# Two attention loops: ScalarE copies every sum, the shift rows lie on 16 partitions, the odd steps' maxima are turned in the 21st unit, and the next step's scores are not held back

## What is computed

```
q = layer_norm(latents) @ Wq
k, v = split(concat([layer_norm(context), layer_norm(latents)], axis=1) @ Wkv)
weight = softmax(q @ k.T * scale)      # the second layer masks some of the 1601 context rows
out = (weight @ v) @ Wout
x = x + out
```

## Time and profile before

| what | value |
|---|---|
| profiled execution, device time | 2073.62 us |
| its span, first to last instruction | 2071.9 us |
| around the span | 1.7 us |
| TensorE busy | 1933.7 us, 93% |
| VectorE busy | 1679.5 us, 81% |
| ScalarE busy | 1238.3 us, 60% |
| GpSimd busy | 858.2 us, 41% |
| granted TensorE clock, mean over the span | 0.972 |

### The profile page before, as it was taken

The page is one execution under the profiler, slowest core; times in us unless marked ns, Lnnn a source line. Parts: engine busy times, 40 slices in busy tenths (PEclk is TensorE's granted clock), DMA queues, the critical chain, the costliest instruction groups (busy, mean ns, idle before and its releaser), DMA issues. The chain is left out here.

```text
span 2071.9 us, 34568 instructions
## 1 busy us (share of the span) xinstructions
PE 1933.7 (93%) x12154; PEld 1052.6 (51%) x12154; DVE 1679.5 (81%) x3987; ACT 1238.3 (60%) x2218; POOL 858.2 (41%) x926
## 2 busy tenths in 40 slices
PE   7899999999999999889898999999999999999886
PEld 6444545444454544533666544454545454544575
DVE  6789898898989897599656888878797979785657
ACT  4366666666657576444224676868777777776212
POOL 4586565666656651088001414343232323231014
PEclk9899999999999999989998999999999999999898
DMA  4322322222222220133105011121121211110100
GB/s 120 108 74 60 92 80 68 67 68 67 67 67 79 51 67 1 32 109 109 40 1 126 14 38 39 42 47 38 38 45 36 55 38 38 38 30 1 29 1 11
DMA packets 148853, 110.51 MB, mean 53 GB/s; under 512 B 120892, under 2 KB 136232, under 8 KB 148680
## 3 DMA queue, kind: packets, MB, share of 16 engines
q1 hardware_dynamic: 148680, 108.31, 19.2%
HBM read 65.15 MB, written 14.29 MB: 38 GB/s over the span
## 5 line engine op out<-in xcount | busy, mean ns | idle before, releaser
L1256 DVE TENSOR_TENSOR x_p_lo<-x_psum,x_p_hi 128x512 f16<-128x512 f32 (+1 forms) x864 | 584.9, 684 | 113.0 <-ACT x_psum L1023 112.1
L1022 ACT ACTIVATE x_p_hi<-x_psum 128x512 f16<-128x512 f32 (+1 forms) x448 | 268.2, 599 | 263.9 <-PE x_psum L857 214.0
L1022 ACT ACTIVATE x_p_hi<-x_psum,x_bcol 128x512 f16<-128x512 f32 (+1 forms) x416 | 290.0, 697 | 152.0 <-PE x_psum L857 150.1
L883 PE MATMUL x_psum<-x_p_hi,x_x_both 128*128 128x512 f16 (+1 forms) x832 | 317.3, 381 | 30.4 <-DVE x_p_lo L1256 29.5
L855 PE MATMUL x_psum<-x_q,x_xT_both 128*128 128x512 f16 x832 | 317.3, 381 | 4.1 <-DMA x_q<-x_shift_rows 4.1
L857 PE MATMUL x_psum<-x_q,x_xT_both 128*128 128x512 f16 x832 | 316.6, 381 | 0.0
L856 PE MATMUL x_psum<-x_q,x_xT_both 128*128 128x512 f16 x832 | 316.6, 380 | 0.0
L884 PE MATMUL x_psum<-x_p_lo,x_x_both 128*128 128x512 f16 (+1 forms) x832 | 315.8, 380 | 0.0
L885 PE MATMUL x_psum<-x_p_hi,x_x_both 128*128 128x512 f16 (+1 forms) x832 | 315.6, 379 | 0.0
L1195 DVE CUSTOM_DVE_ANT_0 x_junk<-x_psum,x_brow 128x512 bf16<-128x512 f32 (+2 forms) x512 | 279.8, 586 | 9.2 <-PE x_psum L941 7.1
L1198 DVE TENSOR_REDUCE x_mx<-x_psum 128x1 f32<-128x512 f32 (+2 forms) x512 | 276.8, 584 | 4.4 <-PE x_psum L941 3.4
(11 more groups left out here) (473 smaller groups left out, 3517.0 us busy)
## 6 DMA issues: line engine op xcount, KB each, us to landing
x_x_both<-context_rows SPq DMA_DIRECT2D x32, 832.0 KB, 5.4
context_rows<-x_x SPq DMA_DIRECT2D x16, 832.0 KB, 3.5
x_raw<-in_ctx SPq DMA_DIRECT2D x16, 768.0 KB
ssm_c_row<-ssm_bc_rows SPq DMA_DIRECT2D x16, 512.0 KB, 4.2
ssm_b_wide<-ssm_bc_rows SPq DMA_DIRECT2D x7, 512.0 KB, 3.5
x_mrow<-in_mask_BxS_bk SPq DMA_DIRECT2D x16, 200.1 KB
x_Wkv<-in_L_xattn_Wkv SPq DMA_DIRECT2D x4, 512.0 KB, 5.1
x_xT_both<-context_rows SPq DMA_TRANSPOSE x96, 4.0
```

Of the source, the lines that this page charges most:

```text
L883: pe.matmul(out, v_hi, p_hi[r][rows, :], start=start, stop=False)
L1022: act.activation(p_hi[r][rows, :], score[r][rows, :], ACT.Exp, scale=SCORE_UNIT, **bias).then_inc(p_hi_ready, 1)
L1256: v.tensor_tensor(p_lo[r][rows, :], score[r][rows, :], p_hi[r][rows, :], ALU.subtract).then_inc(p_lo_ready, 1)
```

## The change

Four things, all inside `attention_loop`.

1. The copies of sums on VectorE (lines 1273 and 1221) go to ScalarE. Both halves of `sum_c` are copied one after the other at the end of a step, behind the products of units 24 and 25, and the latents' sums in two copies of one bank each, behind the exponentials of units 1 and 2.
2. The shift rows lie on 16 partitions of 128 columns, not on 8 of 256. For that `m8` is made twice side by side, and each of the two DMAs per step (constants out, shift rows in) becomes two of half the size.
3. `TURN_BY` is `LAST` - 6 in place of `LAST` - 4. By the rule in `items` an odd step then has two `max` items in units 6 and 7, one in each of units 8 to 19, and `turn` in unit 20. The even step's table is the same as before.
4. The next step's scores 0, 1 and 2 are issued in units 24, 25 and 26, one in each, ahead of the products.

```diff
-    HOLD = 2
-    TURN_BY = LAST - 4
+    TURN_BY = LAST - 6
...
             def rows_in(at):
                 sp.wait_ge(shift_ready, at.n + 1)
-                sp.dma_start(row_of(q_all[at.npar]), shift_rows[:, :, :, :].rearrange("c s h k -> c (s h k)")).then_inc(shift_in, 16)
+                for s in range(2):
+                    sp.dma_start(row_of(q_all[at.npar], s), side(shift_rows, s)).then_inc(shift_in, 16)
...
-                    elif at.has_next and u > LAST - AHEAD + HOLD:
-
-                        k = u + AHEAD - STEPS
-                        for k in range(0 if k == HOLD else k, k + 1):
-                            scores(k, at.npar, at.half + STEPS, at.n, at.ni)
+                    elif at.has_next:
+                        scores(u + AHEAD - STEPS, at.npar, at.half + STEPS, at.n, at.ni)
...
+            def latents_sums(done, par, k):
+                act.wait_ge(pv_done, done)
+                act.activation(sum_l[:, 8 * k:8 * k + 8, par, :], aux[:, k * HALF:(k + 1) * HALF].rearrange("p (h l) -> p h l", l=L),
+                               ACT.Copy).then_inc(aux_free, 1)
...
                     probabilities(u, at)
+                    if at.b and u in (1, 2):
+                        latents_sums(at.half, 1 - at.par, u - 1)
...
-                act.wait_ge(pv_done, at.half + 2 * KT - 1)
-                act.activation(sum_c[:, 0:8, at.par, :], acc[0].rearrange("p (h l) -> p h l", l=L), ACT.Copy).then_inc(sum_out, 1)
+                for k, done in enumerate((sum_out, sum_out1)):
+                    act.wait_ge(pv_done, at.half + 2 * KT - 1 + k)
+                    act.activation(sum_c[:, 8 * k:8 * k + 8, at.par, :], acc[k].rearrange("p (h l) -> p h l", l=L), ACT.Copy).then_inc(done, 1)
...
                         v.wait_ge(aux_free, at.free(item))
-                        v.tensor_reduce(m8[:, :], mx[:, :, :], AX.X, ALU.max).then_inc(m_ready, 1)
+                        for s in range(2):
+                            v.tensor_reduce(m8[:, s, :], mx[:, :, :], AX.X, ALU.max).then_inc(m_ready, 1)
...
-                    if u == 1 and not (at.first and at.par == 0):
-                        latents_sums(at.half, 1 - at.par)
```

More of the change, by code:

```diff
@@ L563, in attention_loop @@
     warm = sb("warm", [P, 1])
-    mx, m8 = sb("mx", [P, NC_, 4]), sb("m8", [P, NC_])
-    const_rows = sb("const_rows", [NC_, 2, 2, P], F16)
-    shift, shift_rows = sb("shift", [NC_, 2, P]), sb("shift_rows", [NC_, 2, 2, P], F16)
+    mx, m8 = sb("mx", [P, NC_, 4]), sb("m8", [P, 2, NC_])
+    const_rows = sb("const_rows", [2 * NC_, 2, P], F16)
+    shift, shift_rows = sb("shift", [2 * NC_, P]), sb("shift_rows", [2 * NC_, 2, P], F16)
     if masked:
@@ L760, in load_mask, with row_of, side @@
                 sp.dma_start(mcol[par][0:TAIL, CT:KT], one[CT * P:S].rearrange("(p o) -> p o", o=1)).then_inc(mask_in[par], 16)
-            def row_of(q):
-                return q[P - 1:P, :, :]
+            def row_of(q, s):
+                return q[P - 1:P, :, 2 * P * s:2 * P * (s + 1)]
+            def side(rows, s):
+                return rows[NC_ * s:NC_ * (s + 1), :, :].rearrange("c h k -> c (h k)")
             def rows_out(at):
@@ L950, in aux_item @@
                         keep_clock(pe, aux[:, 512:1024], ident, 14)
-                    pe.wait_ge(m_ready, at.n + 1)
-                    ins = pe.transpose(aux[0:NC_, 0:P], m8[:, :], ident[:, :])
+                    pe.wait_ge(m_ready, 2 * at.n + 2)
+                    ins = pe.transpose(aux[0:2 * NC_, 0:P], m8[:, :, :].rearrange("p s c -> p (s c)"), ident[:, :])
                 elif kind == "out":
@@ L1036, in body @@
                     wait_alone(act, sum_parted, 2 * (at.b - 1))
-                act.wait_ge(pv_done, at.half + 2 * KT - 1)
-                act.activation(sum_c[:, 0:8, at.par, :], acc[0].rearrange("p (h l) -> p h l", l=L), ACT.Copy).then_inc(sum_out, 1)
+                for k, done in enumerate((sum_out, sum_out1)):
+                    act.wait_ge(pv_done, at.half + 2 * KT - 1 + k)
+                    act.activation(sum_c[:, 8 * k:8 * k + 8, at.par, :], acc[k].rearrange("p (h l) -> p h l", l=L), ACT.Copy).then_inc(done, 1)
             every(act, before, body)
+            for k in range(2):
+                latents_sums(B * STEPS, 1, k)
         @block.gpsimd
@@ L1200, in consume @@
                     if a == (10 if isinstance(at, Pre) else 1 if at.npar else 2 * NC_ - 3):
-                        v.wait_ge(const_in, (at.n + 1) * 16)
-                        v.tensor_tensor(shift[:, :, :], const_rows[:, :, 0, :], const_rows[:, :, 1, :],
-                                        ALU.add).then_inc(const_ready, 1)
+                        v.wait_ge(const_in, (at.n + 1) * 32)
+                        v.tensor_tensor(shift[:, :], const_rows[:, 0, :], const_rows[:, 1, :], ALU.add).then_inc(const_ready, 1)
                     if a == 2 * NC_ - 1:
                         v.wait_ge(aux_free, at.free(item))
-                        v.tensor_reduce(m8[:, :], mx[:, :, :], AX.X, ALU.max).then_inc(m_ready, 1)
+                        for s in range(2):
+                            v.tensor_reduce(m8[:, s, :], mx[:, :, :], AX.X, ALU.max).then_inc(m_ready, 1)
                 elif kind == "turn":
@@ L1211, in consume @@
                     if not (isinstance(at.n, int) and at.n == 0):
[L1212 to L1215, removed]
+                        v.wait_ge(shift_in, at.n * 32)
+                    turned = aux[0:2 * NC_, 0:P]
+                    v.tensor_tensor(shift_rows[:, 0, :], shift[:, :], turned, ALU.subtract)
+                    v.tensor_tensor(shift[:, :], shift[:, :], turned, ALU.subtract).then_inc(aux_free, 2)
                     v.wait_ge(aux_free, at.free(item))
[L1217 to L1221, removed]
+                    v.tensor_tensor(shift_rows[:, 1, :], shift[:, :], shift_rows[:, 0, :], ALU.subtract).then_inc(shift_ready, 1)
             def project(a, at, ready, pair, used=None):
@@ L1268, in body @@
                             consume(at, item)
[L1270 to L1273, removed]
             every(v, before, body)
-            latents_sums(B * STEPS, 1)
             k = base_items(PAIRS, 0, False) - EVEN_ITEMS
```

4 lines of the change are left out of this document (2 added, 2 removed).

## The result

The changed kernel takes 2110.7 us (median of 4 runs, 2107.7 to 2111.2), the kernel before beside it 2071.7 (4 runs): 1.018 times as long, with a 95% interval of 1.016 to 1.020. That is 39.0 us slower, where 30 were forecast, and inside the forecast range of 2078 to 2118.

A forecast was written before the change was run, and what follows sets the result against it. TensorE was taken to set the pace, VectorE close behind. Terms of +22 (two-item units), -9 (odd end), +6 (even end) and +11 (sums on ScalarE) gave +30 on 2073.6, so 2104 us, range 2078 to 2118.

The forecast's parts named there:

- two-item units: Units 6 and 7 of odd steps, two `max` items each: 1.6 us lost per odd step, 14 times, +22 us.
- odd end: End of odd steps: waits of 0.57 us for `p_lo` and 0.10 for shift rows go, 14 times, -9 us.
- even end: End of even steps: score 2 waits 0.6 us for `p_lo` 26; +0.65 masked, +0.2 unmasked, 7 each, +6 us.
- the query item: First query item, unit 1 of unmasked odd steps: its 0.48 us wait for VectorE's latents' copy goes, 7 times.
- sums on ScalarE: Step starts: exp 0 stands behind the second sum copy, so products 0 wait 0.5 us, masked 0.7; +11 us.
- second `m8`, constants' sum: Second `m8` reduction adds at most 0.1 us before `turn`, constants' sum saves up to 0.2; taken as zero, +-3 us.
- The walk: Timing of units 6 and 7, unmasked odd step, from both engines' queues: 1.6 us lost per odd step.
- the stretch of `max` items: Odd step before the change: no TensorE wait there, TensorE and VectorE both full at 1.67 us per unit.
- VectorE the pacer: Rival: VectorE paces the loops and the change frees it, so boundary waits go, 2052 us; chance 0.08.
- The signs to look for: Expected in the profile after: waits of second `max` items, products 0 and score 2, longer odd steps, none on shift rows.
- products 0: First products of even steps: wait 0.5 us (masked 0.7) for a `p_lo` that follows two sum copies.
- a whole transfer later: Rival: the second shift-row DMA lands 5.63 us after `turn`, +19 us, 2123 us; chance 0.08.

The follow-up runs named there:

- b_turn20: Kernel before with only `TURN_BY` = `LAST` - 6, so two `max` items in units 6 and 7: 2090.9 us, 1.009 times the kernel before.
- b_free: Kernel before with only the next step's scores not held back, turn still in unit 22: 2106.1 us, 1.017 times the kernel before.
- a_order: Changed kernel with the second half of `sum_c` copied on ScalarE behind exp 0 of the next step, not ahead: 2095.0 us, 1.011 times the kernel before.
- a_vector: Changed kernel with the copies of sums put back on VectorE: 2099.7 us, 1.014 times the kernel before.
- a_held: Changed kernel with the next step's first three scores held back to unit 26, as before: 2083.4 us, 1.006 times the kernel before.
- a_turn22: Changed kernel with `TURN_BY` = `LAST` - 4 put back, so turn in unit 22: 2124.9 us, 1.026 times the kernel before.
- b_rows16: Kernel before with only the shift rows on 16 partitions and two DMAs: 2077.2 us, 1.0025 times the kernel before.

## Why the prediction was right, and where it was off

**The sum.** Forecast +30, measured +39.0 by medians (34 to 41 by the interval of the ratio) and +35.6 in the 28 steps of the trace. Term by term:

| term | forecast | measured | from |
|---|---|---|---|
| two-item units | +22 | +24.3 | 7 x 1.57 and 7 x 1.9, b_turn20 |
| odd end | -9 | -9.4 | 0.57 and 0.10 gone in 14 steps |
| even end | +6 | +6.1 | b_free: 0.67 in 14 steps; in the unmasked layer less the 0.47 of the query item, 7 times |
| sums on ScalarE | +11 | +14.3 | 12.2, the changed kernel less a_order, and 0.3 that a_order keeps over a_vector in 7 masked even steps |
| second `m8`, constants' sum | 0 | +0.4 | a_held: even steps 0.09 longer in the unmasked layer, 0.03 shorter in the masked one, 7 each |

This makes 35.7, for the 35.6 of the 28 steps. What lies outside the 28 steps is 2.0 us longer in this pair of profiles, less than it varies from run to run.

**Two-item units.** The walk gave 0.95 and 0.4 us for the second items; the rows have 0.94 and 0.38. It was made in the unmasked layer and carried to the masked one, where each maximum is another operation and the pair of units costs 0.3 more per step: this term was too small by 2 us. Products 6 do wait (0.69) where the prediction says that the stretch of `max` items has no wait at all, but its walk starts from that wait, so the sum is not touched.

**The odd end.** The size is right, and the part that it is put down to is not. The prediction booked the -9 on scores that are no longer held back. b_turn20 holds them back and loses 0.50 of the 0.67 all the same, since the earlier turn alone takes the shift operations and the rows away from the end. a_held, with parts 1 to 3, loses the last 0.16 too. What part 4 alone does at the odd end is a wait of 1.97 us on the rows. That the term came out although part 4 alone makes the odd end longer is luck: the forecast took parts 3 and 4 together.

**The even end.** Score 2 waits 0.58 for a forecast of 0.6, in both layers. The unmasked layer's 0.2 holds once the query item's wait is counted with it, and for the reason given: in b_free products 1 stay 6.47 us behind the last `out` item (6.50 before).

**ScalarE.** The mechanism is as forecast, and this is the other term that was too small, by 3 us. The waits are 0.41 in unit 0 for a forecast of 0.5; masked 0.55 and 0.20 for 0.7 and 0.2. Not foreseen were 0.05 to 0.2 in units 3 and 4 of even steps, where `max` items wait for VectorE's maxima, and 0.28 more in unit 1 of unmasked odd steps. The copies off VectorE won nothing beyond the query item, as forecast: with VectorE the pacer, a_vector would have been the slower one.

**The signs to look for.** "Unmasked odd steps about 1.5 us longer, masked ones 1.8" was wrong: they are 0.72 and 1.1 longer by the means, because the list left out the waits at the odd end that its own sum takes off. The others came as written: score 2, products 0, no wait on the rows in unit 24. The rows land 3.76 us after `turn` (a_turn22) and not 4.30: the DMA is issued 1.18 after `turn` for 1.57, since the shift operations took 0.27 us, and from the first issue to the scores are 2.58 for 2.73. So the second DMA does not land a whole transfer later, and that rival falls.

**The parts alone** make -2.5, +5.2, +18.9 and +35 us by their ratios, 57 together, against 38 of the whole by its ratio; in the 28 steps 50.6 against 35.6. Part 3 takes away the wait on the rows that part 4 makes (1.97 in 14 steps, 27.6 us) and with it the steps of lower clock in b_free (6.6). Against that, part 4 makes the copies of part 1 cost 14.3 us where they cost nothing, and parts 3 and 4 each take off waits at the odd end that can go only once (0.50 in 14 steps, 7.0). Part 2 costs 2.2 alone and 0.4 in the whole. These make 14.7 of the 15.0.

## What to carry over

Look at what an engine's queue holds behind a waiting instruction: the same copy was free, useful or dear as the first exponential of the next step stood behind it or ahead of it. Where an item is moved earlier by pairing two of them in a unit, work out that unit on both engines; if both are full, as they were here, nothing gives the loss back. And two DMAs in place of one cost their second issue where the first reader is already waiting: 0.65 us in b_rows16, nothing in the changed kernel, where the rows are in time.

## What the hardware showed

A wait of some 2 us on TensorE cost more than itself in some steps. Windows of a_turn22, from the score 0 that had waited 2.13 us to the end of that step, and from there on:

```profile
674.62:681.83 7.21, 7.21 (x22) 2.21 (x22) 0.69 (x1) 3.17 (x6) 4.17 (x4) 0.55 0.00 0
681.83:690.00 8.17, 8.17 (x40) 3.73 (x39) 6.65 (x18) 7.23 (x14) 2.47 (x10) 0.98 0.33 71
```

The granted clock (the number before the DMA share) is 0.55 over the first stretch, so most of it is at the lower level, 1.2 GHz, though TensorE works without a pause; over the second it is 0.98, nearly all at 2.4 GHz. That step took 54.45 us, where steps of the same kind without it took 51.35. It happened in 5 of 14 odd steps of a_turn22 and in 3 of 14 of b_free and not in the others with the same wait, and in none of the changed kernel's 28 steps, whose longest wait is 1.43; why in these steps, no run here shows. And a VectorE operation that takes 0.18 us alone took 1.22 while GpSimd was adding; behind it stood 1.09 us of TensorE's waiting in each unmasked odd step, the longest wait inside the steps of before.
